# A transformer decoder layer on one core: the fifth exponential ahead of the first output copy, and the first sequence begun one group sooner

## What is computed

```python
x = _layernorm(x + _L0_attn_ref(x, w_qkv, b_qkv, w_proj, b_proj), axis=-1)    # 16 heads of 16, causal
x = _layernorm(x + _L0_xattn_ref(x, ctx, ctx, w_q, w_k, w_v, w_o), axis=-1)   # 16 heads of 64, 77 keys
x = _layernorm(x + _L0_ffn_ref(x, k0, k1, k2, s0, s1, s2), axis=-1)           # relu(h @ (+1/-1)) three times, 1024 wide
```

## Time and profile before

| | before |
|---|---|
| median of three runs | 2183.49 us (2180.5 to 2187.31) |
| the profiled execution, its own time | 2188.87 us |
| its span, first to last instruction | 2187.2 us |
| mean granted TensorE clock | 0.991 of full speed |
| PE busy / PEld / DVE / ACT / POOL | 97% / 85% / 69% / 52% / 31% |

### The profile page before, as it was taken

One profiled execution on the slowest core, in us unless ns is written; L12 is line 12 of the kernel. 1 busy time (PEld: TensorE's weight loads), 2 busy tenths in 40 slices (PEclk: granted clock), 3 DMA queues, 4 the chain that ended last, 5 costly groups with the idle time before them and its releaser, 6 DMA issues.

```text
span 2187.2 us, 54589 instructions
## 1 busy us (share of the span) xinstructions
PE 2113.9 (97%) x18572; PEld 1869.4 (85%) x18572; DVE 1500.9 (69%) x4647; ACT 1133.0 (52%) x2571; POOL 669.5 (31%) x751
## 2 busy tenths in 40 slices
PE   8998789999999999999999999999999999999998
PEld 7887678888888888888888888888888888888887
DVE  5554467777777777777777777777777777777764
ACT  5554445555555554555555555555555555555553
POOL 2000222333333333333333333333333333333331
PEclk9999899999999999999999999999999999999999
DMA  8997533233323333322333233333223332333310
GB/s 257 310 295 229 127 74 68 66 63 72 74 51 73 77 77 77 77 66 65 63 72 73 52 73 77 77 77 77 65 65 64 72 71 54 73 77 77 77 44 10
DMA packets 180579, 196.57 MB, mean 90 GB/s; under 512 B 50130, under 2 KB 135154, under 8 KB 180466
## 3 DMA queue, kind: packets, MB, share of 16 engines
q1 hardware_dynamic: 180532, 195.94, 38.6%
HBM read 69.37 MB, written 58.87 MB: 59 GB/s over the span
## 4 chain that ended last, share of the span: by engine, by line
PE 83%; ACT 6%; issue 4%; DVE 4%; DMA 1%; POOL 1%; SPq 1%; ACTq 0%; POOLq 0%; DVEq 0%
PE ps L1204 13%; PE ps L1387 11%; PE ps L1245 9%; PE ps L1246 9%; PE ps L1353 5%; PE ps L1281 5%; PE ps L1213 4%; PE ps L1296 3%; PE ps L1228 3%; PE ps L1185 3%; PE ps L1270 3%; PE ps L1154 3%; PE ps L1371 3%; PE ps L1168 2%; ACT probs L653 2%
## 5 line engine op out<-in xcount | busy, mean ns | idle before, releaser
L1245 PE MATMUL ps<-r_h,w 128*128 128x256 f16 x2048 | 461.8, 273 | 1.6 <-DVE r_l L845 1.6
L1246 PE MATMUL ps<-r_l,w 128*128 128x256 f16 x2048 | 460.6, 273 | 0.0
L859 DVE CUSTOM_DVE_ANT_0 junk<-ps,causal 128x128 bf16<-128x128 f32 (+1 forms) x1024 | 331.3, 356 | 125.8 <-PE ps L1270 114.9
L505 POOL TENSOR_SCALAR_AFFINE_SELECT probs<-probs 128x512 f32<-128x512 f32 x256 | 163.0, 637 | 459.7 <-ACT probs L653 455.3
L528 POOL TENSOR_TENSOR rstd<-var_eps,minus_half 128x2 f32<-128x2 f32 x96 | 66.7, 694 | 671.1 <-DVE var_eps L834 671.1
L628 ACT ACTIVATE p2r<-ps,low 128x77 f32<-128x77 f32 x1024 | 242.1, 338 | 44.0 <-DVE low L898 43.2
L519 POOL TENSOR_TENSOR p<-p2r,inv 128x308 f32<-128x308 f32 x256 | 201.1, 786 | 197.2 <-DVE inv L909 193.5
L1387 PE MATMUL ps<-vo_h,p2t 128*128 128x256 f32 (+1 forms) x1280 | 239.3, 290 | 8.0 <-DVE p2t L916 8.0
L1245 PEld LDWEIGHTS ps<-r_h,w 128*128 128x128 f16 x2048 | 200.2, 98 | 35.7 <-issue 9.5
L591 ACT ACTIVATE r_h<-ps 128x512 f16<-128x512 f32 x256 | 148.8, 597 | 154.3 <-PE ps L1246 139.2
L845 DVE SCALAR_TENSOR_TENSOR r_l<-ps,r_h 128x512 f16<-128x512 f32 x256 | 172.9, 687 | 75.3 <-ACT r_h L591 75.2
(11 more groups left out here) (145 smaller groups left out, 4742.7 us busy)
## 6 DMA issues: line engine op xcount, KB each, us to landing
vo_scratch<-vo_out SPq DMA_DIRECT2D x80, 448.0 KB, 5.1
vo<-vo_scratch SPq DMA_DIRECT2D x64, 512.0 KB
q_st<-p2t SPq DMA_DIRECT2D x192, 128.0 KB
k_bd<-p2t SPq DMA_DIRECT2D x192, 128.0 KB, 6.0
q<-q SPq DMA_DIRECT2D x128, 128.0 KB, 2.1
k_bd<-k_scratch SPq DMA_DIRECT2D x64, 154.0 KB, 3.6
x_in<-in_x SPq DMA_DIRECT2D x32, 256.0 KB, 2.7
out<-y SPq DMA_DIRECT2D x32, 256.0 KB, 6.4
```

The lines of the kernel that those rows point to most:

```text
L859: dve.tensor_tensor_reduce(out=junk[:, e, b * P:b * P + width], in0=ps[:, bank + b, e * width:(e + 1) * width], in1=causal[:, (1 - b) * P: ...
L1245: pe.matmul(dst, w1[:, kk, m * P:(m + 1) * P], r0_h[:, kk, :], start=kk == 0, stop=False)
L1246: last = pe.matmul(dst, w1[:, kk, m * P:(m + 1) * P], r0_l[:, kk, :], start=False, stop=kk == KF - 1)
```

## The change

Three edits. On ScalarE, in every pass, `self_probs(i, 4)` goes ahead of `self_output(i, 0)`. In the first phase, on all engines, the start of the first sequence moves one group sooner: its load behind group (4, 0), its transposes to (4, 1), its queries and keys to (4, 2) and (4, 3), its values and the stacks of queries and keys to (4, 4) to (4, 6); the transposes of the last context tile move from j = 1 to j = 0. The begin of its scores stays at (5, 2). In the last sequence's `layer1` each of the first four steps waits for the low part that it reads itself, where the first three waited for three; the loop over the parts of `layer2` is written out in the same order.

```diff
--- before.py
+++ after.py
@@ -437,15 +437,15 @@
                     elif g:
                         save_value_outputs(g - 1, KX - 1)
                     save_keys(g, j)
-                    if (g, j) == (4, 1):
+                    if (g, j) == (4, 0):
                         sp.wait_ge(w_bin, 4)
                         sp.dma_start(x_in[:], x[0].rearrange("(b p) d -> p b d", p=P)).then_inc(x_loaded, 16)
-                    if (g, j) == (4, 5):
+                    if (g, j) == (4, 4):
                         sp.wait_ge(zero_saved, 16)
                         query_stacks_begin(0)
+                    if (g, j) == (4, 5):
+                        query_stacks_end(0)
                     if (g, j) == (4, 6):
-                        query_stacks_end(0)
-                    if (g, j) == (4, 7):
                         key_stacks(0)
                     if (g, j) == (5, 6):
                         stack_max(0, 0)
@@ -673,8 +673,8 @@
                     transposed_x2(f)
                 if more:
                     queries_keys(i + 1, 0)
+                self_probs(i, 4)
                 self_output(i, 0)
-                self_probs(i, 4)
                 self_probs(i, 5)
                 self_probs(i, 6)
                 if more:
@@ -742,14 +742,14 @@
                     elif g:
                         value_outputs_out(g - 1, KX - 1)
                     keys_out(g, j)
-                    if j == 1 and g + 1 < NG:
+                    if j == (0 if g == 4 else 1) and g + 1 < NG:
                         ctx_high(g + 1)
+                    if (g, j) == (4, 1):
+                        transposed_x(0, 0)
                     if (g, j) == (4, 2):
-                        transposed_x(0, 0)
-                    if (g, j) == (4, 3):
                         act.wait_ge(small_in, 16 * 10)
                         queries_keys(0, 0, 1)
-                    if (g, j) == (4, 4):
+                    if (g, j) == (4, 3):
                         queries_keys(0, 1, 0)
                     if (g, j) == (5, 6):
                         negated_max(0, 0, (0, S))
@@ -1080,15 +1080,15 @@
                         value_outputs_out(g, j - 1)
                     elif g:
                         value_outputs_out(g - 1, KX - 1)
-                    if j == 1 and g + 1 < NG:
+                    if j == (0 if g == 4 else 1) and g + 1 < NG:
                         ctx_low(g + 1)
-                    if (g, j) == (4, 2):
+                    if (g, j) == (4, 1):
                         dve.wait_ge(const_pool, N_CONST)
                         transposed_x(0, 0)
-                    if (g, j) in ((4, 3), (4, 4)):
-                        for m in (2 * j - 6, 2 * j - 5):
-                            queries_keys(0, m, 4 - j)
-                    if (g, j) == (4, 5):
+                    if (g, j) in ((4, 2), (4, 3)):
+                        for m in (2 * j - 4, 2 * j - 3):
+                            queries_keys(0, m, 3 - j)
+                    if (g, j) == (4, 4):
                         self_values(0, 1)
                     if g == 5 and j >= 2 and j != 6:
                         self_max(0, j - 2 - (j > 6), 0)
@@ -1230,12 +1230,12 @@
                 if m % 2:
                     last.then_inc(pe_z0, 1)
 
-            def layer1(f, q):
+            def layer1(f, q, last_banks=False):
 
                 m, part = q // 4, q % 4
                 u = m // 2
                 if q < 4:
-                    pe.wait_ge(d_r0, nth(f, 4, max(q + 1, 3)))
+                    pe.wait_ge(d_r0, nth(f, 4, q + 1 if last_banks else max(q + 1, 3)))
                 if q == 8:
                     pe.wait_ge(d_r0, nth(f, 4, 4))
                 if q % 8 == 0 and u >= 2:
@@ -1525,19 +1525,19 @@
                     elif g:
                         value_outputs(g - 1, KX - 1)
                     context_keys(g, j)
-                    if j == 1 and g + 1 < NG:
+                    if j == (0 if g == 4 else 1) and g + 1 < NG:
                         ctx_transposes(g + 1)
 
-                    if (g, j) == (4, 2):
+                    if (g, j) == (4, 1):
                         pe.wait_ge(a_ct, NG)
                         pe.wait_ge(d_ct, NG)
                         transposed_inputs(0, 0)
-                    if (g, j) == (4, 3):
+                    if (g, j) == (4, 2):
                         pe.wait_ge(w_low[3], 4)
                         queries_keys(0, 0, 1)
+                    if (g, j) == (4, 3):
+                        queries_keys(0, 1, 0)
                     if (g, j) == (4, 4):
-                        queries_keys(0, 1, 0)
-                    if (g, j) == (4, 5):
                         self_values(0, 1)
                     if (g, j) == (5, 2):
                         pe.wait_ge(const_pool, N_CONST)
@@ -1569,10 +1569,12 @@
             pe.wait_ge(d_y3, nth(B - 2, 2, 2))
             for m in range(KF):
                 layer0(B - 1, m, LAST_BANKS)
-            layer1_until(B - 1, 0, 4 * KF)
-            for blocks in (range(0, 6), range(6, KF)):
-                for b in range(TB):
-                    layer2(B - 1, b, blocks, 6)
+            for q in range(4 * KF):
+                layer1(B - 1, q, last_banks=True)
+            layer2(B - 1, 0, range(0, 6), 6)
+            layer2(B - 1, 1, range(0, 6), 6)
+            layer2(B - 1, 0, range(6, KF), 6)
+            layer2(B - 1, 1, range(6, KF), 6)
 
 
 # ---- launch: one core; inputs and outputs as the reference has them ----
```

## The result

| | before | after |
|---|---|---|
| median of four runs each | 2183.28 us (2180.5 to 2187.31) | 2214.76 us (2213.61 to 2216.86) |
| ratio, 95% interval | | 1.014 (1.0128 to 1.0153) |
| span of the profiled execution | 2187.2 us | 2215.1 us |
| mean granted TensorE clock of it | 0.991 | 0.989 |

The change costs 31.5 us between the medians. Slower was forecast, but by 13, and the time lies above the range. The new wait came where it was forecast, and it is nearly twice as long (0.80 us for 0.45). The page's engine line hardly moves against the earlier trace rows: PE has 3.4 us more of busy time in a span that is 28 longer.

The account below looks back on a forecast made before the run. TensorE, busy 97%, was taken as the bound, so any added wait is paid in full. Swap +14.7, last layer 1 -0.7, first phase -1.0 gave +13.0 us: 2197 us, own range 2188 to 2206, widened to 2181 to 2207.

Parts of the forecast that it names:

- The exponential gains nothing by going first: ScalarE, each pass: the fifth exponential waits for PE's scores, so moving it gains 0, at most 0.08 us.
- Copy, transfer and reciprocal 1.41 us later: Each pass: output copy starts 1.41 us later; its transfer still lands in 2.1 us, so DVE's reciprocal moves equally.
- The rival in which the transfers get shorter: Packing transfer lands in 1.65 instead of 2.1 us, so the delay is covered: 2181.8 us, chance 0.12.
- The product at 0.42 us: VectorE L889, each pass: product starts at 1033.03 and ends at 1033.45, its length unchanged.
- The term 0.45 us a pass: PE waits for the first L845 before layer 0's fifth block: 0.45 us lost per pass, 13.1 us in 29.
- no second wait: Second L845 ends at 1035.45, before PE needs the second bank at 1035.78, so PE does not wait again.
- The last pass: Copy moves 1.53 us with no cover ahead of L845: 1.2 us lost, between 0.9 and 1.5.
- Part 2: Last sequence's layer 1: taking the four L845 one by one starts the last four matmuls sooner, -0.7 us.
- Part 3: First phase one group sooner: stacked keys' wait goes, a `vo_out` copy wait comes; net -1.0 us, -4.0 to +0.9.
- Covered: Rival: L845 ends less than 0.38 us later, so PE never notices the delay; 2181.8 us, chance 0.12.
- faster: Rival: ScalarE's queue released the exponential, so the seventh score tile's 0.33 us wait goes; 2171.9 us, chance 0.08.
- the fall of the clock in the loop: Rival: the new wait lowers TensorE's granted clock in each pass, +51 us in 30 passes; 2248 us, chance 0.05.

Follow-up runs that it names:

- e5: Kernel before with the change's last layer 1, and on TensorE layer 0's second block moved ahead of the seventh score tile: 2172.37 us, ratio 0.9942.
- e3: Changed kernel with GpSimd's eighth mask of each pass replaced by a fill of the same block with ones: 2199.82 us, ratio 1.007.
- e8: Changed kernel with the swap and the last layer put back, leaving only the first phase one group sooner: 2188.07 us, ratio 1.0015.
- e7: Changed kernel with GpSimd's eighth mask of each pass waiting until VectorE's product is done: 2211.5 us, ratio 1.0122.

## Why the prediction was wrong

**The exponential gains nothing by going first: right.** It starts at the same place, and the wait that hangs on it is 9.0 for 8.9 us. e5 says what would have helped.

**Copy, transfer and reciprocal 1.41 us later: right** to 0.01 us, the transfer's 2.1 us included. The rival in which the transfers get shorter did not come.

**The product at 0.42 us: the step that failed.** The prediction took its length from the trace as the instruction's own and carried it to another moment, without looking who else works at that moment. The product was forecast for 1033.03 to 1033.45, and the mask that releases PE at 1033.66 ran from 1032.97 to 1033.61. Of masks the prediction asked only whether they would be late for PE, never whether they would stand beside VectorE's work. The trace of before held the warning too, 0.52 us in the first pass. The term 0.45 us a pass became 0.86, in 29 passes 11.8 us of the 18.3 by which 2214.76 lies above the forecast's 2196.5. With the mask's effect taken off (e3) the pass is the 60.6 us of the forecast, so the rest of this chain was right: the place (L845 ahead of the fifth block), the 0.45 us, and no second wait.

The Trainium skill, "SBUF — State Buffer", section "Who interferes with whom", says: "A DVE instruction with two SBUF inputs contends with a GpSimd instruction that reads SBUF", and that one which only writes it is no hindrance. The runs agree with this for the mask: the product reads two operands in SBUF and ends 0.28 us after the mask in every alignment; beside a fill that only writes, it takes its 0.43. The section also says, of VectorE's two-port modes, that whoever issues first has the shared ports for its whole instruction while the other is blocked. The runs fit a product that waits for the mask's end and by then has some 0.14 us of its 0.42 behind it, since it ends 0.28 us later. They don't show that every reader hinders it: in the last pass of before GpSimd's small operation L528 (128x2), which reads SBUF too, ran from 0.20 us ahead of the product to 0.07 behind its end (GpSimd's spans are rough), and the product took 0.43. That L528 reads 2 elements a partition and the mask 512 may be why; no run tried it.

**The last pass: right in kind, too low.** 1.2 us were taken, between 0.9 and 1.5. PE's wait at L1228 went from 0.34 to 2.04. SyncE, VectorE and TensorE there:

```profile
2136.42 0.62 SPq L338 DMA_DIRECT2D q<-q  x1
2137.10 1.54 SPq L339 DMA_DIRECT2D q<-q  x1
...
2139.54 1.75 DVE L886 RECIPROCAL q<-q 128x256 f32<-128x256 f32 x1 [4.17 <-DMA q<-q]
2141.40 0.43 DVE L889 TENSOR_TENSOR q<-q 128x256 f32<-128x256 f32 x1
...
2142.49 0.39 PE L1228 MATMUL ps<-x2t_h,w 128*128 128x256 f16 x2 [2.04 <-DVE r_l L845]
```

No mask runs beside the product, and it takes 0.43. What is different is the transfer: its issue at 2136.42 is followed by the reciprocal 3.12 us later, where it was 2.16 in the last pass of before (2108.20 to 2110.36), and the second issue takes 1.54 us on SyncE for 0.61 in the loop. The view of the DMA queues shows, in this stretch (packets, MB, share of the 16 engines), a transfer of instructions, of which the loop has none:

```profile
q1 hardware_dynamic: 288, 0.26, 10.0%
q8 instruction: 1, 0.02, 1.0%
```

It lies in the last pass of before too, where the second transfer was the late one (the 0.64 us of the earlier trace rows). That it holds the first one up after the change is a guess, and no run tried it. It is not the swap's doing alone: at least one of these two transfers lands late in all ten kernels, in four without the swap the second (3.8 to 4.0 us), in the five with it both (2.7 to 3.1 us), and in e5, which has no swap, both as well (2.8 and 2.9). The stretch to the end has 1.27 us more in sum; with the 0.7 us that part 2 gives back, the last pass costs 2.0.

**Part 2: right**, -0.7.

**Part 3: wrong in sign, a small term.** The keys' wait went, as forecast, and the wait for the copy of `vo_out` took its place, as forecast, but it was put at 2.3 us and is 3.6. The last context tile's wait came out at 3.23 us, not 4.3, but 0.83 of the wait for `x` stayed, and nothing was won back at the clock: the slow stretch from 169 us is gone, but after the new wait the clock stands at 0.74 for 8.2 us (0.79 in the same stretch before), and over 152 to 225 us it is 0.95 in both traces. The changed kernel's stretch (length, busy us by engine, clock, DMA share, GB/s; below it the loop):

```profile
201.60:209.80 8.20, 8.20 (x53) 7.35 (x54) 4.09 (x18) 3.04 (x6) 0.00 (x0) 0.74 0.64 203
425.00:2100.00 1675.00, 1630.24 (x14515) 1445.83 (x14516) 1200.66 (x3843) 867.06 (x2049) 569.04 (x631) 1.00 0.34 70
```

**The rivals.** Covered and faster did not come. Nor did the fall of the clock in the loop: it stands at 1.00 with a wait of 0.81 us added to each pass.

**The range** was made of bounds on the terms that were in the sum. None stood for an instruction that takes longer than it did, and that alone carried the time above it. (Added up again, the bounds give 2187 to 2205 in place of 2188 to 2206, and part 3's upper end is +0.8; nothing hangs on it.) Of the 18.3 us missed, 11.8 are the product, 4.3 part 3 (by e8, 2.3 to 6.2) and 0.8 the last pass; the remaining 1.4 stay open and are less than part 3's uncertainty.

## What to carry to other kernels

When an edit moves an instruction in time, look at what every other engine does in the stretch where it will stand, and read its length from a place in the trace where it has the same neighbours: here one instruction was forecast to 0.01 us in its start and came out at twice its length. The pair that mattered here is VectorE with two operands in SBUF beside a GpSimd operation that reads a large block of it. And where PE waits for another engine whose own input comes from PE, give PE other work in the gap before reordering the other engine's queue: that was worth 0.37 us a pass (e5), the reordering cost 0.86.

## What the runs showed of the hardware

- A product of two SBUF tiles on VectorE (128x256, f32) takes 0.42 us alone and up to 0.86 beside GpSimd's mask of 128x512 that began first, which itself keeps its 0.64. Beside a fill of the same block it takes 0.43.
- The one time that the product began first (e8, first pass, 0.20 us ahead of a mask), the product kept its 0.43 us and the mask took 0.72 in place of 0.64.
- GpSimd's small operation behind the mask (L528) took 0.86 us in the changed kernel, where the lengthened product was still running as it began, and 0.69 in e7, where it was not.
- An added wait shortened a pass: e7's wait on GpSimd takes 0.23 us off.
- The same SyncE issue took 0.61 us in the loop and 1.54 in the last pass.
